# Filler matmuls on TensorE before four waits of the last stages left out, in a Perceiver layer on one core

## The chip, the core and the metric

The kernel runs on one core of a Trainium2 chip. The metric is the device time of one execution in microseconds (us), as the median of several executions. The profile is of one more execution, taken by the hardware profiler; its times are counted from the start of its span.

## What is computed

One layer on a state x of 128 rows x 512 columns and a context of 12544 rows x 512:

```
x = x + xattn(layernorm(x), ctx)          # 16 heads of 128, softmax over 12544 keys
x = x + lightning_attn(layernorm(x))      # 16 heads of 32, one chunk of 128 rows
x = x + ffn(layernorm(x))
# lightning_attn:
q, k, v = silu(x@Wq), silu(x@Wk), silu(x@Wv)
o = ((q k^T) * decay) v                   # per head
o = o * sigmoid(x@Wg1@Wg2);  o = rmsnorm per head * norm_w;  return o@Wo
# ffn: both products with ternary weights and rows rounded to 8 bits
h = gelu(silu(act_quant(rms_norm(x)) @ w1q^T + b1))
h = layer_norm(h) * ln_g + ln_b
return act_quant(rms_norm(h)) @ w2q^T + b2
```

## The kernel before, in words

Every engine has its own program, written out by hand, and each instruction that depends on another engine waits on a semaphore. Nothing is scheduled by a planner around the change: the order on TensorE is the order of the text in `block.tensor`.

The first 2017 us of the profile are the cross attention (the key and value products at L1097 and L1119). After it come these stages, all of which hang on one another:

- Heads of the cross attention, 16 times: VectorE normalises a head (L924), TensorE turns it (four f32 transposes, `transposes`, L1061), ScalarE copies it out (L684), TensorE multiplies by Wv (L1174) and Wo (L1181). Weights of the heads come by DMA (`bulk<-in_vo`).
- First norm: VectorE adds the residual (L939) and computes the layer norm with a guess of the reciprocal square root from GpSimd (L754 to L758, L458). TensorE waits for it (`ydone`), turns the result (L1061), ScalarE copies it (L688).
- Lightning attention: the gate's first product (L1206), Q and K (L1213, 64 matmuls of 128x128 f32), the gate's second product (L1217), V (L1220), scores (L1228), scores by V (L1237, 32 matmuls of 32 columns), and the residual put into `ps_c` by a product with the identity (L1240). VectorE then does the gate and the norm per head (L949 to L956). TensorE waits for it (`an_done`), turns the result, ScalarE copies it (L700), and TensorE multiplies by Wo (L1247).
- Third norm: ScalarE copies x2 (L702), VectorE computes the layer norm and rounds the rows to 8 bits (L987 to L979). TensorE waits for it (`f_q`), turns the rows in bf16 (L1061), ScalarE copies (L706), and TensorE multiplies by w1 (L1268, four groups `h_mm` of four matmuls 128x512 bf16). VectorE takes each group (L1003) and works on it with ScalarE: silu, gelu, statistics.
- Fourth norm: VectorE normalises the 2048 columns and rounds them in four parts (L1027 to L979, `h_norm`, `f2_q`). TensorE turns each part (L1061), ScalarE copies it (L724), and TensorE multiplies by w2 (`second`, L1256, 16 matmuls in all). VectorE adds it up (L1051), and the output is stored.

Before each of the four waits TensorE runs filler matmuls. `keep_warm(n)` issues n products of the identity in bf16 with 512 columns of the ternary weights, into the first bank of `ps_s`, which nobody reads before it is written again:

```
def keep_warm(n):
    for _ in range(n):
        mm(ps_s[:, 0:D], identb[:, :], tern[:, 0:D], start=True, stop=True)
```

The four calls: 14 ahead of the wait for `ydone`, 16 ahead of `an_done`, 28 ahead of `f_q`, and 24 behind the first wait for `h_norm`, ahead of the four waits for `f2_q`. They stand at L1196.

Of the kernel before, what the change touches and what calls it, by code (L numbers as in the profile page):

```python
# [6 lines left out]
D = 512  # L7
# [103 lines left out]
def perceiver_layer(nc, x_d, ctx_d, qk_d, vo_d, aw_d, wg1_d, wg2_d, w12_d, ld_d, normw_d, b1_d,  # L111
                    lng_d, lnb_d, b2_d, ident_d, diff_d, mask_d, out_d):
    es = ExitStack()
    with es:
        def sb(name, cols, dt=F32):
            return es.enter_context(nc.sbuf_tensor(name, [P, cols], dt))

        def pb(name, cols):
            return es.enter_context(nc.psum_tensor(name, [P, cols], F32))
# [20 lines left out]
        identb = sb("identb", P, BF16)  # L140
# [30 lines left out]
        tern = bulk[:, 0:WP * D].bitcast(BF16)  # L171
# [27 lines left out]
        def t_moving(k, lo, blk, c):  # L199
            start, stride, n, m, _, _ = window(k)  # L200
            return runs(bulk16, ((lo * 7 + blk) * 2 + c) * TW + start, stride, n, m)
# [9 lines left out]
        ps_s = pb("ps_s", 1024)  # L211
# [30 lines left out]
        def visit(k):  # L242

            return sum(e == STEPS[k][0] for e, _, _ in STEPS[:k])
# [108 lines left out]
        def _(sp):  # L353
# [62 lines left out]
            for k in range(1, NS + 1):  # L416
                turn_p(k - 1, 0)
                turn_p(k - 1, 1)
                for j, (_, _, at) in enumerate(LOADS):
                    if at == k + 1:  # L420
                        load_ctx(j)
                if 0 <= k - ABS_AT + 1 < 2 * WP:
                    load_w(k - ABS_AT + 1)
                if 0 <= k - QUANT_AT + 1 < 2 * WP:
                    load_w(2 * WP + k - QUANT_AT + 1)
                if 0 <= k - QUANT_AT - 1 < 2 * WP:
                    store_w(k - QUANT_AT - 1)
# [628 lines left out]
        def _(pe):  # L1056
            mm = nc.tensor.matmul
# [132 lines left out]
                    add_out(f - 1)  # L1190
            add_out(H - 1)

            def keep_warm(n):

                for _ in range(n):
                    mm(ps_s[:, 0:D], identb[:, :], tern[:, 0:D], start=True, stop=True)  # L1196


            pe.wait_ge(in_tern, 32)
            keep_warm(14)  # L1200
            pe.wait_ge(ydone, 2)
            transposes(ps_t, acc, KC, ident).then_inc(ytp, 1)
            pe.wait_ge(ytc, 2)
            yt = slot(1)
            for c in range(KC):
                last = mm(ps_a[0:AHD, 0:P], wg1[:, c * AHD:(c + 1) * AHD], yt[:, c * P:(c + 1) * P], start=(c == 0),  # L1206
                          stop=(c == KC - 1))
# [11 lines left out]
            for c in range(KC):  # L1219
                last = mm(ps_a[:, :], yt[:, c * P:(c + 1) * P], aw_v[:, c * D:(c + 1) * D], start=(c == 0),  # L1220
                          stop=(c == KC - 1))
# [16 lines left out]
                              slot(7)[:, h * AHD:(h + 1) * AHD], start=True, stop=True)  # L1238
            last.then_inc(ao_mm, 1)
            mm(ps_c[:, :], ident[:, :], x1[:, :], start=True, stop=False)  # L1240
            keep_warm(16)
            pe.wait_ge(an_done, 1)
            transposes(ps_t, slot(14), KC, ident).then_inc(at_mm, 1)
            pe.wait_ge(at_cp, 1)
            pe.wait_ge(in_aw2[2], 16)
            for c in range(KC):
                last = mm(ps_c[:, :], slot(1)[:, c * P:(c + 1) * P], aw_o[:, c * D:(c + 1) * D], start=False,  # L1247
                          stop=(c == KC - 1))
# [3 lines left out]
            def second(n):  # L1252
# [4 lines left out]
                              start=(c == 0), stop=(c == WP - 1), skip_group_check=True)  # L1257
                return last

            keep_warm(28)  # L1260
            pe.wait_ge(f_q, 1)
            transposes(ps_a[:, 0:D // 2].bitcast(BF16), slot(2)[:, 0:D // 2].bitcast(BF16), KC, identb).then_inc(f_tp, 1)
            pe.wait_ge(f_tc, 1)
# [5 lines left out]
                              tern[:, c * F + n * D:c * F + (n + 1) * D], start=(c == 0), stop=(c == KC - 1))  # L1269
                last.then_inc(h_mm, 1)  # L1270
            pe.wait_ge(h_norm, 1)
            keep_warm(24)
            for n in range(4):
                pe.wait_ge(f2_q, n + 1)
                src = slot(12 + n // 2)[:, (n % 2) * D // 2:(n % 2 + 1) * D // 2].bitcast(BF16)
# [61 lines left out]
```

## Time and profile before

| | us |
|---|---|
| median of 3 executions | 2171.31 (2171.03 to 2172.21) |
| the profiled execution's own time | 2166.53 |
| its span | 2164.7 |
| mean granted clock of TensorE over the span | 0.977 |
| TensorE busy | 2063.1 (95%) |
| VectorE busy | 1208.0 (56%) |
| ScalarE busy | 920.0 (42%) |

The granted clock is the share of the full 2.4 GHz: 1.00 is 2.4 GHz and 0.50 is 1.2 GHz. In a timeline a row is a run of like instructions, with its start, its length, and in brackets how long the engine had been idle ahead of it and what ended that. In the chain of waits a row is a piece of the path that ended last. In a table of windows "busy (x)" is the time and the number of instructions in the stretch, one that crosses its edge included. The table gives all of the span; the stages that the change touches lie behind 2087 us.

### The profile page before, as it was taken

How to read it: one execution, taken by the hardware profiler on the slowest of the kernel's cores; microseconds unless marked ns; L12 is line 12 of the kernel's file. 1: busy time of each engine (PE TensorE's matmuls, PEld its weight loads, DVE VectorE, ACT ScalarE, POOL GpSimd, SP SyncE). 2: the span in 40 equal slices, each digit the busy share in tenths (PEclk: the TensorE clock that was granted, in tenths of full speed). 3: DMA queues.
4: the chain of work that ended last, by engine and by line, in shares of the span. 5: the costliest groups of instructions: out<-in, count | busy, mean ns of one | idle time of the engine just before them, and what ended most of it. 6: DMA issues, size and time to landing. Idle time of an engine off the chain costs nothing.

```text
span 2164.7 us, 29322 instructions
## 1 busy us (share of the span) xinstructions
PE 2063.1 (95%) x11200; PEld 1112.1 (51%) x11200; DVE 1208.0 (56%) x2127; ACT 920.0 (42%) x1993; POOL 215.3 (10%) x241
## 2 busy tenths in 40 slices
PE   5599999999999999999999999999999999999686
PEld 4455555555555555555555555555555555555452
DVE  3455555556555556666766756555555565554326
ACT  3343445445454344444444444444444343443212
POOL 4401010001010010100000101010010100100001
PEclk8799999999999999999999999999999999999898
DMA  5243444444434435544545443343434343333730
GB/s 161 69 88 69 95 96 103 92 108 98 103 93 102 93 69 114 102 112 107 105 101 122 109 96 78 83 93 66 94 71 92 70 88 79 83 69 54 256 133 5
DMA packets 516698, 206.74 MB, mean 96 GB/s; under 512 B 418864, under 2 KB 502832, under 8 KB 515664
## 3 DMA queue, kind: packets, MB, share of 16 engines
q1 hardware_dynamic: 516560, 204.88, 41.9%
q8 instruction: 89, 1.46, 0.3%
q14 instruction: 49, 0.40, 0.1%
HBM read 97.59 MB, written 4.46 MB: 47 GB/s over the span
## 4 chain that ended last, share of the span: by engine, by line
PE 90%; DVE 4%; POOL 2%; DMA 2%; issue 1%; ACT 1%; SPq 0%; POOLq 0%; DVEq 0%; ACTq 0%
PE ps_s L1097 22%; PE ps_t L1097 17%; PE ps_b L1119 12%; PE ps_c L1119 12%; PE ps_a L1119 11%; PE ps_u L1119 11%; DMA bulk<-in_vo 1%; POOL acc L477 1%; PE ps_t L1174 1%; POOL stage L477 1%; PE ps_a L1076 0%; DVE pp L810 0%; PE ps_c L1181 0%; DMA acc<-in_qk 0%; PE ps_s L1213 0%
## 5 line engine op out<-in xcount | busy, mean ns | idle before, releaser
L1097 PE MATMUL ps_s<-bulk 128*128 128x384 f16 (+2 forms) x3264 | 579.0, 321 | 3.5 <-issue 3.2
L1097 PE MATMUL ps_t<-bulk 128*128 128x384 f16 (+2 forms) x2448 | 450.5, 321 | 14.9 <-ACT ps_t L638 10.1
L1097 PEld LDWEIGHTS ps_s<-bulk 128*128 128x128 f16 x3264 | 315.3, 98 | 216.5 <-issue 5.1
L477 POOL TENSOR_TENSOR stage<-stage 128x256 f32<-128x256 f32 x196 | 171.2, 873 | 1610.6 <-DMA stage<-in_ctx 1591.8
L1097 PEld LDWEIGHTS ps_t<-bulk 128*128 128x128 f16 x2448 | 233.9, 98 | 168.9 <-ACT ps_t L638 11.6
L638 ACT ACTIVATE ps_t<-ps_s 128x384 f32<-128x384 f32 (+2 forms) x136 | 62.9, 462 | 488.7 <-PE ps_s L1097 488.7
L1119 PE MATMUL ps_b<-nring,pt 128*128 128x512 f16 x1176 | 264.9, 379 | 1.0 <-DMA pt<-pp 1.0
L1119 PE MATMUL ps_u<-nring,pt 128*128 128x512 f16 x1176 | 265.0, 379 | 0.0
L1119 PE MATMUL ps_c<-nring,pt 128*128 128x512 f16 x1176 | 264.9, 379 | 0.0
L1119 PE MATMUL ps_a<-nring,pt 128*128 128x512 f16 x1176 | 264.9, 379 | 0.0
L810 DVE SCALAR_TENSOR_TENSOR pp<-prob,pp 128x768 f16<-128x768 f32 (+2 forms) x272 | 257.2, 987 | 0.1
L855 DVE TENSOR_TENSOR ps_t<-ps_t,part_e 128x384 f32<-128x384 f32 (+2 forms) x136 | 74.8, 550 | 244.9 <-PE ps_t L1097 244.8
L659 ACT ACTIVATE pp<-prob 128x768 f16<-128x768 f32 (+2 forms) x272 | 207.1, 812 | 3.0 <-DMA pt<-pp 3.0
L1119 PEld LDWEIGHTS ps_a<-nring,pt 128*128 128x128 f16 x1176 | 115.1, 98 | 138.8
L1119 PEld LDWEIGHTS ps_c<-nring,pt 128*128 128x128 f16 x1176 | 115.0, 98 | 138.9 <-DMA pt<-pp 0.3
L1119 PEld LDWEIGHTS ps_b<-nring,pt 128*128 128x128 f16 x1176 | 114.9, 98 | 132.4 <-DMA pt<-pp 1.5
L1119 PEld LDWEIGHTS ps_u<-nring,pt 128*128 128x128 f16 x1176 | 115.0, 98 | 131.2 <-DMA pt<-pp 0.3
L832 DVE SCALAR_TENSOR_TENSOR acc<-acc,alpha,ps_c 128x512 f32<-128x512 f32 x64 | 47.8, 748 | 194.1 <-PE ps_c L1119 194.1
L832 DVE SCALAR_TENSOR_TENSOR acc<-acc,alpha,ps_a 128x512 f32<-128x512 f32 x64 | 47.8, 747 | 192.8 <-PE ps_a L1119 192.8
L633 ACT ACTIVATE prob<-ps_s,nmax 128x768 f32<-128x768 f32 (+2 forms) x72 | 61.4, 853 | 194.4 <-DVE nmax L803 180.0
L799 DVE TENSOR_REDUCE mx<-ps_s 128x1 f32<-128x768 f32 (+2 forms) x136 | 126.0, 926 | 4.7
L799 DVE TENSOR_REDUCE mx<-ps_t 128x1 f32<-128x768 f32 (+2 forms) x136 | 125.0, 919 | 0.0
(185 smaller groups left out, 1600.0 us busy)
## 6 DMA issues: line engine op xcount, KB each, us to landing
stage<-in_ctx SPq DMA_DIRECT2D x392, 128.0 KB, 2.5
wst<-in_w SPq DMA_DIRECT2D x64, 256.0 KB, 3.3
acc<-in_qk SPq DMA_DIRECT2D x16, 512.0 KB, 4.6
bulk<-in_vo SPq DMA_DIRECT2D x16, 512.0 KB, 4.9
pt<-pp SPq DMA_TRANSPOSE x272, 4.0
tern_d<-wter SPq DMA_DIRECT2D x32, 128.0 KB, 3.1
bulk<-tern_d SPq DMA_DIRECT2D x2, 2048.0 KB, 16.1
nring<-in_aw SPq DMA_DIRECT2D x3, 1024.0 KB, 12.8
```

The lines of the kernel that those rows point to most:

```text
L477: nc.gpsimd.tensor_tensor(piece(t, dst), piece(t, a), piece(t, b), op).then_inc(done, 1)
L633: nc.scalar.activation(prob_of(k, g), scores_of(k, g), ACT.Exp, bias=nmax_of(k, g), scale=EXP_SCALE, accum_out=total).then_inc(exp_done[g], 1)
L638: nc.scalar.activation(bank_b(k), bank_a(k), ACT.Copy).then_inc(a_copied, 1)
L659: nc.scalar.activation(pp_part(k, g, 0), prob_of(k, g), ACT.Copy, scale=P_SCALE).then_inc(hi_done[g], 1)
L799: nc.vector.reduce_max(mx[:, g:g + 1], scores_of(k, g), AX.X).then_inc(mx_done, 1)
L810: nc.vector.scalar_tensor_tensor(pp_part(k, g, 1), prob_of(k, g), P_SCALE, pp_part(k, g, 0), ALU.mult, ALU.subtract).then_inc(lo_done[g], 1)
L832: nc.vector.scalar_tensor_tensor(slot(h), slot(h), alpha[:, h:h + 1], bank_u(k, g)[:, :], ALU.mult, ALU.add).then_inc(acc_done[g], 1)
L855: nc.vector.tensor_tensor(bank_d(k), bank_b(k), part_e[:, 0:cols(k)], ALU.add).then_inc(d_done, 1)
L1097: ins = mm(out, q_part(e, qlo, a)[:, c * P:(c + 1) * P], t_moving(k, tlo, b, c), start=(first and c == 0 and qlo == 0 and tlo == 0), stop= ...
L1119: ins = mm(bank_u(k, g)[:, :], pt[:, tile:tile + P], n_part(c, clo, half), start=(n == 0 and half == 0 and plo == 0 and clo == 0), stop=(n ...
L1174: last = mm(ps_t[:, (f % 2) * D:(f % 2) * D + HD], w[:, c * HD:(c + 1) * HD], ut[:, (f % 2) * D + c * P:(f % 2) * D + (c + 1) * P], start= ...
```

## The change

`keep_warm` and its four calls are left out. The waits, and all other instructions, stay in their order on every engine.

```diff
@@ -1190,14 +1190,7 @@
                     add_out(f - 1)
             add_out(H - 1)
 
-            def keep_warm(n):
-
-                for _ in range(n):
-                    mm(ps_s[:, 0:D], identb[:, :], tern[:, 0:D], start=True, stop=True)
-
-
             pe.wait_ge(in_tern, 32)
-            keep_warm(14)
             pe.wait_ge(ydone, 2)
             transposes(ps_t, acc, KC, ident).then_inc(ytp, 1)
             pe.wait_ge(ytc, 2)
@@ -1238,7 +1231,6 @@
                               slot(7)[:, h * AHD:(h + 1) * AHD], start=True, stop=True)
             last.then_inc(ao_mm, 1)
             mm(ps_c[:, :], ident[:, :], x1[:, :], start=True, stop=False)
-            keep_warm(16)
             pe.wait_ge(an_done, 1)
             transposes(ps_t, slot(14), KC, ident).then_inc(at_mm, 1)
             pe.wait_ge(at_cp, 1)
@@ -1257,7 +1249,6 @@
                               start=(c == 0), stop=(c == WP - 1), skip_group_check=True)
                 return last
 
-            keep_warm(28)
             pe.wait_ge(f_q, 1)
             transposes(ps_a[:, 0:D // 2].bitcast(BF16), slot(2)[:, 0:D // 2].bitcast(BF16), KC, identb).then_inc(f_tp, 1)
             pe.wait_ge(f_tc, 1)
@@ -1269,7 +1260,6 @@
                               tern[:, c * F + n * D:c * F + (n + 1) * D], start=(c == 0), stop=(c == KC - 1))
                 last.then_inc(h_mm, 1)
             pe.wait_ge(h_norm, 1)
-            keep_warm(24)
             for n in range(4):
                 pe.wait_ge(f2_q, n + 1)
                 src = slot(12 + n // 2)[:, (n % 2) * D // 2:(n % 2 + 1) * D // 2].bitcast(BF16)
```

## Rows read from the trace of the kernel before

**Rows 1.** Chain of waits behind 2087 us: start, us, engine, tile, line, count

```profile
2091.34 0.67 PE ps_t L1061 x4
...
2093.74 7.34 PE ps_s L1213 x64
...
2108.51 4.41 PE ps_u L1237 x32
...
2121.70 3.71 PE ps_c L1247 x8
...
2133.93 1.92 PE ps_s L1268 x8
...
2135.87 0.75 DVE acc L1003
...
2139.12 0.75 DVE acc L1003
...
2159.30 0.40 PE ps_s L1061 x4
2159.69 1.74 PE ps_c L1256 x8
```

**Rows 2.** Timeline of TensorE behind 2087 us: fillers and what follows them

```profile
2087.31 3.19 PE L1196 MATMUL ps_s<-bulk,identb 128*128 128x512 bf16 x14
...
2114.57 5.38 PE L1196 MATMUL ps_s<-bulk,identb 128*128 128x512 bf16 x16
...
2125.23 6.21 PE L1196 MATMUL ps_s<-bulk,identb 128*128 128x512 bf16 x28
2132.85 0.40 PE L1061 MATMUL ps_a<-identb,acc 128*128 128x128 bf16 x4 [1.41 <-DVE acc L979]
...
2147.87 7.50 PE L1196 MATMUL ps_s<-bulk,identb 128*128 128x512 bf16 x24 [10.31 <-DVE acc L1035]
2155.34 0.40 PE L1061 MATMUL ps_t<-identb,acc 128*128 128x128 bf16 x4
2156.66 0.40 PE L1061 MATMUL ps_t<-identb,acc 128*128 128x128 bf16 x4 [0.92 <-DVE acc L979]
```

**Rows 3.** Timeline of TensorE: idle stretches without fillers, elsewhere in the kernel

```profile
75.59 0.51 PE L1097 MATMUL ps_t<-bulk 128*128 128x128 f16 x6 [2.24 <-DVE ps_t L855]
...
124.57 3.79 PE L1097 MATMUL ps_s<-bulk 128*128 128x384 f16 x12 [3.17 <-issue]
...
2021.35 1.25 PE L1061 MATMUL ps_s<-ident,un 128*128 128x128 f32 x8 [3.85 <-DVE un L924]
...
2025.81 1.12 PE L1061 MATMUL ps_s<-ident,un 128*128 128x128 f32 x4 [0.98 <-DVE un L924]
...
2067.57 2.08 PE L1174 MATMUL ps_t<-ut,bulk 128*128 128x128 f32 x8 [7.23 <-DMA bulk<-in_vo]
...
2077.89 1.06 PE L1174 MATMUL ps_t<-ut,bulk 128*128 128x128 f32 x8
```

**Rows 4.** Windows of TensorE: us, PE busy (count), granted clock, DMA share, GB/s

```profile
77.00:78.00 1.00, 0.04 (x1) 0.50 0.65 131
...
124.60:125.00 0.40, 0.40 (x2) 0.67 0.00 0
...
128.00:129.00 1.00, 1.00 (x7) 0.92 0.77 204
...
2022.00:2023.00 1.00, 0.81 (x6) 0.77 0.97 410
...
2073.60:2073.80 0.20, 0.20 (x3) 0.63 1.09 430
...
2111.20:2111.40 0.20, 0.20 (x3) 0.74 0.00 0
...
2142.00:2142.20 0.20, 0.00 (x0) 0.54 0.00 0
...
2152.20:2152.40 0.20, 0.20 (x2) 0.86 0.00 0
```

## The prediction

> **What bounds the kernel now.** I first read the chain of waits behind 2087 us [rows 1]: to 2121.70 it goes through TensorE's own products (Q and K 7.34 us, scores by V 4.41 us, the product by Wo 3.71 us), later through VectorE with TensorE answering, and at the end through TensorE again (1.74 us for the last eight products). No filler stands in it. The timeline says why [rows 2]: the 14 fillers end at 2090.5, the 16 at 2119.95 and the 28 at 2131.44, each before its wait ends (the transposes of the third norm have 1.41 us of idle ahead of them, behind the fillers). Only the 24 last ones touch their successor: 2147.87 + 7.50 = 2155.37 against transposes at 2155.34. So the fillers cost next to nothing, and the question is what they hold up: the clock. The windows [rows 4] show the granted clock at one of two levels, 1.00 (2.4 GHz) or 0.50 (1.2 GHz).
>
> **How the clock falls.** A stop is the start of a row less its idle time. TensorE stopped at 73.35 and was idle 2.24 us [rows 3]; at 77.00 the clock was 0.50 [rows 4]. It stopped at 121.40, was idle 3.17 us [rows 3], and the mean of 0.67 between 124.60 and 125.00 [rows 4] puts the fall at 124.74, 3.3 us after the stop. It stopped at 2017.50, was idle 3.85 us [rows 3], and the mean of 0.77 from 2022 to 2023 [rows 4] puts the fall at 2022.54, 5.0 us after the stop and behind eight transposes. It stopped at 2137.56, which is 10.31 us ahead of 2147.87 [rows 2], and the clock fell at 2142.02 [rows 4], 4.5 us later. Not one of these idle times was survived.
>
> **How it rises.** Work began at 124.57 and the clock rose at 128.16, 3.6 us later; at 2067.57, rose at 2073.75, 6.2 us; at 2147.87 (the fillers themselves), rose at 2152.26, 4.4 us [rows 2 to 4]. I take the middle one, 4.4 us, and 3.6 and 6.2 as bounds. At 1.2 GHz the same eight products take 2.08 us against 1.06 [rows 3], so of 4.4 us half, 2.2 us, are lost (bounds 1.8 and 3.1). Four f32 transposes take 1.12 us at the low clock [rows 3] against 0.67 [rows 1]: 0.45 us more.
>
> **The change part by part.** It removes 82 matmuls with their weight loads, adds and moves nothing; the other engines' programs are the same, no DMA is touched, and the waits stay. Without the fillers the four idle stretches are:
>
> *First norm.* Idle from about 2087.4 (start of the fillers) to 2091.34 [rows 1, 2], 3.9 us, as long as the 3.85 us above [rows 3]. By the rows the fall comes 3.3 to 5.0 us after the stop, so before or after the transposes: I take half of 0.45, 0.2 us. Then come the gate's product and 64 of Q and K, without a pause, and the chain is TensorE's own: 2.2 us. **2.4 us**, bounds 1.8 and 3.5 if it falls at all.
>
> *Scores by V.* These 32 small products cost 4.41 us, and the clock falls at 2111.30 [rows 4], 2.8 us into them. At the full clock they would take 2.8 + 1.6/2 = 3.6 us, at the low one 7.2. The stage arrives later than before, and where the fall then comes no row shows. I take **0**, since the same products lead up to it; bounds -0.8 and +2.8.
>
> *Norm per head.* Idle over 5.4 us (the length of the 16 fillers) [rows 2], ahead of it those small products, with the clock already low: low for certain when work returns. The transposes cost 0.45 and the product by Wo 2.2: at the low clock throughout it would take some 3.5 us more, and it is on the path. **2.6 us**, bounds 2.2 and 4.0.
>
> *Third norm.* Idle 7.6 us (2125.23 to 2132.85) [rows 2], more than any of the stops survived. The four bf16 transposes take 0.40 us where f32 ones take 0.67, so I put them at half of 0.45: 0.2. VectorE reads the second group at 2135.87 as soon as eight matmuls from 2133.93 are done [rows 1]. The 28 fillers in 6.21 us give 0.22 us for one at 2.4 GHz, hence 0.43 at 1.2: eight are 1.7 us late. The last group is read only at 2139.12, and with the clock back after 4.4 us it is ready by then, so the later groups add nothing. **1.9 us**, bounds 1.7 and 2.7 (all sixteen at the low clock are ready 2 us after 2139.12).
>
> *Fourth norm.* Idle from 2137.56 to 2155.34. Here the fillers started cold too, and had the clock up 3 us before the rows came. Without them the first transposes (0.2 us late) are covered by VectorE, which gives the next part only at 2156.66. From there three blocks of transposes (0.5 us each at the low clock) and 16 products at 0.43 make 8.3 us of low-clock work, up to 2165 instead of 2161.4: 3.6 us if the clock stays low. If it rises 4.4 us after 2155.34, 5.4 us of this work are left and run in 2.7, end 2162.5; if 4.4 us after 2156.66, 3.9 are left, end 2163.0. **1.3 us**, bounds 0.9 and 3.6.
>
> **The sum** is 2.4 + 0 + 2.6 + 1.9 + 1.3 = 8.2 us. The profiled execution took 2166.53 us, so its like would take 2174.7. The median of the runs stands 4.8 us above it, at 2171.31; none of the four stages waits for a DMA, so I carry the sum over unchanged: **2179.5 us**.
>
> **The rivals.** *The clock survives the first norm.* Its idle is the shortest of the four, and the stop of 3.85 us [rows 3] kept the clock for 5.0 us. Then that term is gone: 5.8 us, 2177.1. Against it, there too the clock fell a moment later, and 2.24 us of idle sufficed at 73.35. Chance 0.17.
>
> *The clock comes back late or not at all in each stage.* The work there is short and broken by transposes and waits, and the 6.2 us of 2067.57 had transposes within. Then 3.5 + 0 + 4.0 + 2.4 + 3.6 = 13.5 us, 2184.8. Beside this stands a rule of the Trainium skill ("TensorE: Matmul & The Clock Gate", Part 4: PE-mode transpose): the full clock does not engage for transposes, which do not count as a busy TensorE in the same way. By that rule the last stage, in which transposes alternate with products, would be nearer to its 3.6 us than to my 1.3. The rise at 2073.75 came after a stretch with transposes in it, so the trace does not bear out the strong form. Chance 0.12.
>
> *Not slower.* In the last stage the fillers end at 2155.37 and the transposes wait for them. Where the clock rises 6.2 us after the restart instead of 4.4, the 24 fillers end 0.9 us later and hold up the path by as much, and leaving them out gives that back. This decides if the clock is still at 2.4 GHz when work returns in the other three stages, so that they lose nothing: 2170.4 to 2171.3. For it speaks only that a fall can come 5.0 us after a stop; against it are idle times of 5.4 and 7.6 us. Chance 0.06.
>
> *The low clock is mostly hidden*, because VectorE or ScalarE is late anyway in the last two stages and the rise comes early: 3 to 4 us, some 2175. The chain through TensorE [rows 1] speaks against it. Chance 0.05.
>
> **How the numbers follow.** The forecast keeps 0.60. The range leaves out the last two cases and the upper half of the late clock, together 0.17, and takes in the bounds of the terms where they don't all fall on one side: 2175.5 to 2183.0. A measurement of this kernel can tell about 0.2%, 4.3 us, from no change, that is 2175.6. Slower by more: nearly all of the forecast (0.58) and of the first rival (0.15), and the late clock (0.12): 0.85. Within 0.2%: the rest of those, the hidden case and most of the not-slower one: 0.13. Faster: 0.02.
>
> **What would show it.** In the profile of the changed kernel the granted clock should be 0.50 at the start of the Q and K products, of the product by Wo, of the product by w1 and of the last stage; the eight products by the attention's Wo should take about 6 us instead of 3.71, the Q and K products about 9.5 instead of 7.34, and VectorE should wait some 1.7 us longer for the second group of the product by w1. VectorE's own stretches between (the norms) should keep their length, and everything ahead of 2087 us its place. I am wrong if the clock is 1.00 at those places, if it is low and the stages still keep their length, or if the difference arises ahead of the first norm.

## The result and the profile after

The changed kernel takes 2175.57 us (median of 20 executions, 2172.68 to 2180.84) against 2171.03 us (20, 2168.47 to 2173.02) on the same chips: ratio 1.0023, 95% interval 1.0016 to 1.0030, which is 3.5 to 6.5 us slower. The forecast was 2179.5 us (8.2 us slower), with a range of 2175.5 to 2183.0: the measured median lies 3.9 us below the forecast and only 0.07 us inside the lower end of the range. The profiled execution of the changed kernel took 2173.32 us (span 2171.5 us) against 2166.53.

Ahead of 2087 us the programs are the same, and what differs there is the execution: the first head's transposes start 1.8 us later (2023.12 against 2021.35) and the first norm 0.9 us later (2088.41 against 2087.51). In all profiles of kernels that are alike up to there, the first norm starts between 2087.49 and 2090.84. Behind it the chain of waits of the kernel after reads as follows. The columns are start, length, engine, tile, line; L1206 was L1213, L1230 was L1237, L1239 was L1247, L1248 was L1256.

```profile
2092.34 0.64 PE ps_t L1061 x4
...
2093.65 1.91 PE ps_a L1199 x8
2095.57 8.05 PE ps_s L1206 x64
...
2111.05 4.18 PE ps_u L1230 x32
...
2122.65 1.13 PE ps_t L1061 x4
...
2124.46 5.33 PE ps_c L1239 x8
...
2141.86 0.75 DVE acc L1003
...
2162.65 0.61 PE ps_t L1061 x4
2163.26 1.71 PE ps_c L1248 x4
...
2165.39 0.87 PE ps_c L1248 x4
...
2166.49 1.74 PE ps_c L1248 x8
```

Against [rows 1], Q and K take 8.05 us instead of 7.34, the small products of the scores 4.18 instead of 4.41, the product by Wo 5.33 instead of 3.71, and the first four products by w2 1.71, twice their later 0.87. VectorE reads the second group of the product by w1 4.63 us behind the start of the turn, instead of 3.02. The timeline of TensorE shows the idle time that the fillers had covered, in brackets, against [rows 2]:

```profile
2092.34 0.63 PE L1061 MATMUL ps_t<-ident,acc 128*128 128x128 f32 x4 [3.96 <-DVE acc L758]
...
2122.65 1.12 PE L1061 MATMUL ps_t<-ident,acc 128*128 128x128 f32 x4 [5.58 <-DVE acc L956]
...
2137.23 0.61 PE L1061 MATMUL ps_a<-identb,acc 128*128 128x128 bf16 x4 [7.46 <-DVE acc L979]
...
2161.42 0.58 PE L1061 MATMUL ps_t<-identb,acc 128*128 128x128 bf16 x4 [17.87 <-DVE acc L979]
```

And the windows of TensorE (us, busy and count, granted clock, DMA share, GB/s) show the clock as in [rows 4]:

```profile
2093.50:2094.00 0.50, 0.35 (x2) 0.61 0.00 0
2097.00:2097.50 0.50, 0.50 (x6) 0.98 0.00 0
2124.00:2125.00 1.00, 0.54 (x1) 0.50 0.00 0
2127.50:2128.00 0.50, 0.50 (x2) 0.76 0.00 0
2137.00:2139.00 2.00, 0.68 (x5) 0.50 0.00 0
2141.00:2141.50 0.50, 0.50 (x3) 0.60 0.00 0
2161.00:2163.00 2.00, 0.93 (x8) 0.50 0.00 0
2165.00:2165.50 0.50, 0.50 (x6) 0.71 0.00 0
```

The clock is at 1.2 GHz from 2093.6 to 2097.0, from before the return of work at 2122.65 to 2127.7, and likewise to 2141.4 and to 2165.3: once in each of the four stages. (The moment of a fall or a rise is worked out from the mean clock of the window that it lies in.)

To compare executions I divide the stretch from the start of VectorE's residual add (L939) to the start of its last sum (L1051) at VectorE's results. Four pieces move, and the rest (the first norm, the norm per head and the third norm) is 17.8 us in every profile:

- attention: end of the first norm to VectorE's gate (Q and K, V, scores, small products)
- Wo: end of the norm per head to the statistics of x2 (turn, copy, product, copy)
- w1: third norm's rounded rows to the first rounded part of the fourth norm (VectorE's work of that norm included)
- last: from there to the last sum

| kernel (one profile each) | attention | Wo | w1 | last | whole stretch |
|---|---|---|---|---|---|
| before | 21.74 | 5.76 | 22.48 | 6.25 | 74.02 |
| before_again | 23.61 | 5.76 | 23.78 | 6.24 | 77.20 |
| after | **23.14** | **7.84** | **24.11** | **7.04** | 79.91 |
| after_again | **26.24** | **7.76** | **24.06** | **7.03** | 82.89 |
| no_first | **23.59** | 7.47 | 23.78 | 6.24 | 78.87 |
| no_second | 21.76 | **9.26** | 23.58 | 6.24 | 78.65 |
| no_third | 21.79 | 5.76 | **24.42** | 6.24 | 76.01 |
| no_fourth | 21.40 | 7.46 | 23.96 | **7.41** | 78.03 |
| turned_fill | 23.92 | 5.77 | 24.15 | 6.24 | 77.86 |
| heads_fill | 22.06 | 5.77 | 23.77 | 6.24 | 75.64 |
| heads_fill3 | 23.17 | 5.77 | 22.48 | 6.24 | 75.44 |
| full_fill | 21.95 | 6.22 | 22.49 | 6.25 | 74.70 |
| late_loads | 23.21 | 5.77 | 22.49 | 6.24 | 75.50 |
| late_all | 23.77 | 6.02 | 22.49 | 6.24 | 76.31 |

Bold: the piece has no fillers ahead of it. The stretches of after and before differ by 5.9 us; with the 0.9 us ahead of it, that is the 6.8 us between their profiled executions. The expectations below count some pieces from the turn's start instead: 21.68 us there is 21.74 here, 5.08 is 5.76 (with ScalarE's copy), 3.02 lies within the 22.48.

### The profile page after: what moved, and what is told of

Its sections match the earlier page's. It is cut to its first block, busy times and chain, and to the rows that moved or that the text cites. A ratio compares the mean times of both kernels' runs of the same rounds, so it can differ in the third digit from the quotient of the medians.

```text
span 2171.5 us, 29159 instructions
## 1 busy us (share of the span) xinstructions
PE 2048.8 (94%) x11117; PEld 1108.5 (51%) x11118; DVE 1207.4 (56%) x2127; ACT 919.3 (42%) x1993; POOL 214.3 (10%) x241
## 4 chain that ended last, share of the span: by engine, by line
PE 91%; DVE 3%; POOL 2%; DMA 2%; issue 1%; ACT 1%; SPq 0%; POOLq 0%; DVEq 0%; ACTq 0%
PE ps_s L1097 23%; PE ps_t L1097 17%; PE ps_b L1119 12%; PE ps_c L1119 12%; PE ps_u L1119 11%; PE ps_a L1119 11%; DMA bulk<-in_vo 1%; POOL acc L477 1%; PE ps_t L1174 1%; POOL stage L477 1%; PE ps_a L1076 0%; DMA acc<-in_qk 0%; PE ps_c L1181 0%; PE ps_s L1061 0%; PE ps_s L1206 0%
```

## The experiments

**One call left out at a time.** Each is the kernel before less one line. For no_first it is this one; for no_second, no_third and no_fourth it is `keep_warm(16)`, `keep_warm(28)` and `keep_warm(24)`.

```diff
-            keep_warm(14)
```

> Only the 14 fillers ahead of the first norm's wait are left out. Clock theory: idle of 3.9 us, the granted clock falls about when the transposes run and comes back 3.4 us later, so the stretch from the transposes to the gate (21.68 us before) takes 1 to 2 us more, and the other three stages keep their lengths (5.08, 3.02 and 6.25 us); the time is 1 to 2 us above before. Rival (the fillers matter by something other than the clock): the clock stays 1.00 and the stretch is still longer, or the loss turns up in a later stage.

> Only the 16 fillers ahead of the wait for the norm per head are left out. Clock theory: the piece from the transposes to the copy of x2 takes 7.1 us instead of 5.08 (transposes 1.12, product by Wo 5.3 us), +2.0 us in all, and the 28 fillers behind it restore the clock, so that the next stages keep their lengths. Rival: the piece keeps its length, or the loss is carried on into the third norm as well.

> Only the 28 fillers ahead of the third norm's wait are left out. Clock theory: VectorE reads the second group of the product by w1 1.6 us later (4.6 us behind the transposes' start instead of 3.0), the groups behind it add nothing, +1.6 us in all. Rival: sixteen matmuls at the low clock make the last group late, too: +2 us or more.

> Only the 24 fillers behind the first wait for h_norm are left out. Clock theory: the piece from the first rounded part to the last sum of VectorE takes 7.0 us instead of 6.25, +0.8 us; the clock comes back 3 to 4 us after the first transposes. Rival (transposes do not bring the clock back, as my late-clock case had it): the clock stays at 0.50 to the end and the piece is 3 us or more longer.

Measured (ratio to before, 95% interval): no_first 1.0008 (0.9997 to 1.0018), no_second 1.0016 (1.0006 to 1.0025), no_third 1.0002 (0.9992 to 1.0011), no_fourth 1.0006 (0.9996 to 1.0015). Only the second call alone is clear of noise; the four add up to 0.0032, against 0.0023 for all together, within their intervals. In the profiles the stage without its fillers is longer than in the first profile of before in each case (bold in the table), as the clock theory had it: by 1.9, 3.5, 1.9 and 1.2 us. Three of these are more than the theory's own numbers (2.0, 1.6 and 0.8 for the last three). The late clock of my prediction's rival did come in no_second: there it rose at 2128.61 only, so the eight products by Wo took 6.74 us, nearly all at 1.2 GHz. In no_third the clock rose 5.6 us after the first transposes of the stage, and VectorE read the second group 4.93 us after them (expected 4.6); the later groups added nothing. For no_fourth the rival fell: transposes and products together had the clock back 4.6 us after the first transposes (2161.38 to 2165.97), a little later than the 3 to 4 us expected.

But in three of the four the rest of the expectation failed: *other* stages, their fillers in place, did not keep the lengths of the first profile (only no_third has them all). In no_first the product by Wo, with its 16 fillers in place, took 5.40 us. The timeline and the windows of no_first show why:

```profile
2117.13 4.14 PE L1196 MATMUL ps_s<-bulk,identb 128*128 128x512 bf16 x16
2122.91 0.66 PE L1061 MATMUL ps_t<-ident,acc 128*128 128x128 f32 x4 [1.64 <-DVE acc L956]
2124.26 5.40 PE L1246 MATMUL ps_c<-nring,acc 128*128 128x512 f32 x8 [0.69 <-ACT acc L700]
```

```profile
2124.00:2125.00 1.00, 0.74 (x2) 1.00 0.00 0
2125.00:2128.00 3.00, 3.00 (x5) 0.50 0.00 0
2128.00:2129.00 1.00, 1.00 (x3) 0.79 0.00 0
```

The clock had come back about 1 us after these fillers began (3.6 us in before), so the same 16 took 4.14 us instead of 5.38 and ended 1.64 us ahead of the turn; 0.69 us of ScalarE's copy follow behind it, and the clock fell at 2125.0, some 0.75 us into the product. The other profiles bear this out. Of those with 16 fillers there (turned_fill with its transposes included), the two with 1.64 and 1.75 us of idle ahead of this turn (no_first, no_fourth) lost the clock in the product by Wo; the seven with 0.20 to 0.91 us kept it.

**Is that the kernel before, too?** Both kernels again, unchanged.

> The kernel before, unchanged, for a second profile. Theory (the fillers keep the clock only in some executions, since the idle left around them lets it fall too): from VectorE's residual add of the first norm to its last sum this takes more than the 74.0 us of the first profile, 75 to 78 us, with the product by w1 or by Wo at the low clock at its start and the small products of the scores at 4.0 to 6.7 us. Rival (the first profile is typical, the other losses came from the edits): 74.0 to 74.5 us.

> The changed kernel, unchanged, for a second profile. Its stretch from the residual add to the last sum took 79.9 us. Theory: 79 to 82 us here, with each of the four stages low at its start, and the time at low clock in them different from the first profile by up to 2 us a stage. Rival: 79.9 us again within 0.3, stage by stage.

The second profile of before has a stretch of 77.20 us, 3.2 more than the first, and the execution took 2171.13 us; the first took 2166.53. (Other executions of before have a median of 2171.03 us in the comparison with after and of 2169.64 us beside this run.) Of the 4.6 us between the two, 3.2 lie in the stretch and 1.4 ahead of it. Its windows of TensorE, first under the small products of the scores, then at the product by w1 with the 28 fillers ahead of it:

```profile
2111.00:2120.00 9.00, 9.00 (x33) 0.50 0.00 0
...
2137.00:2138.00 1.00, 0.78 (x4) 0.96 0.00 0
2138.00:2141.00 3.00, 3.00 (x9) 0.50 0.00 0
```

and the rows of its timeline there:

```profile
2136.13 0.40 PE L1061 MATMUL ps_a<-identb,acc 128*128 128x128 bf16 x4 [1.42 <-DVE acc L979]
2137.22 2.95 PE L1268 MATMUL ps_s<-bulk,prob 128*128 128x512 bf16 x8 [0.69 <-ACT prob L706]
```

The idle ahead of this turn is that of the first profile (1.41 us in [rows 2]), which kept the clock; this one lost it at 2137.9. The first window shows a second thing: the clock fell at 2110.6, under the 32 small products, which took 6.35 us instead of 4.41. The changed kernel's second profile has a stretch of 82.89 us, all four stages low at their starts, and differs from its first mostly in the attention piece (26.24 against 23.14). Its clock was low from 2092.2 to 2099.1 in the first stage, and rose 7.7 us after the first transposes. The stretch is longer than the 82 us that I had set as the upper end.

**Transposes as fillers.** The filler's 512 columns as four transposes of 128:

```diff
-                for _ in range(n):
-                    mm(ps_s[:, 0:D], identb[:, :], tern[:, 0:D], start=True, stop=True)
+                for i in range(4 * n):
+                    at = i % 4 * P
+                    nc.tensor.transpose(ps_s[:, 0:D // 2].bitcast(BF16)[:, at:at + P], tern[:, at:at + P], identb[:, :])
```

> Each filler matmul is replaced by four bf16 transposes 128x128 (same columns, TensorE as long busy). If transposes hold the clock like matmuls, all four stages keep the lengths of before (21.68, 5.08, 3.02, 6.25 us) and the time is that of before within 1 us. If they do not count (the rule of the Trainium skill, TensorE: Matmul & The Clock Gate, Part 4), the clock falls while they run, the stages take the lengths of the kernel without fillers (22.99, 7.16, 4.63, 7.04), and the time is 4 to 6 us above before.

Ratio 1.0001 (0.9991 to 1.0010). The windows of TensorE in the stretches in which it ran transposes as fillers:

```profile
2119.40:2121.40 2.00, 2.00 (x21) 0.50 0.00 0
2121.50:2122.00 0.50, 0.50 (x9) 0.77 0.00 0
...
2130.00:2137.00 7.00, 6.43 (x113) 1.00 0.01 2
...
2154.40:2159.00 4.60, 4.60 (x45) 0.50 0.00 0
2159.00:2159.50 0.50, 0.50 (x9) 0.72 0.12 33
2159.50:2162.00 2.50, 2.50 (x49) 1.00 0.00 0
```

From 2154.31 on only transposes run, and the clock comes back at 2159.28; from 2130 to 2137 they hold it. So these bf16 transposes count for the clock here, against the rule of the Trainium skill that the prediction weighed ("TensorE: Matmul & The Clock Gate", Part 4: PE-mode transpose). No run has f32 transposes alone. The lengths did not all come out as expected: the attention piece (23.92 us) and the w1 piece (24.15) are the longer ones, as in before_again, from falls at 2111.49 under the small products and at 2138.80 in the product by w1. The Wo piece and the last one have the lengths of before.

**Fillers led up to the ends of the waits.**

```diff
-            keep_warm(14)
+            keep_warm(17)
             pe.wait_ge(ydone, 2)
             transposes(ps_t, acc, KC, ident).then_inc(ytp, 1)
+            keep_warm(2)
...
             keep_warm(16)
+            pe.wait_ge(lna, 3)
+            keep_warm(6)
             pe.wait_ge(an_done, 1)
             transposes(ps_t, slot(14), KC, ident).then_inc(at_mm, 1)
+            keep_warm(2)
...
-            keep_warm(28)
+            keep_warm(33)
```

with two more behind the turn of the third norm.

> Before, with the fillers led up to the end of each wait (17 instead of 14; 6 more behind GpSimd's guess for the norm per head; 33 instead of 28) and two more behind each turn, while ScalarE copies. Theory: the clock is 1.00 through the product by Wo and the product by w1 in the profile (5.8 and 3.1 us for the two pieces), the stretch takes 74 to 76 us, what is left being the small products of the scores, and the time is 1 to 2 us below before. Rival: the clock still falls there, or the fillers themselves hold up the turns, and the time is that of before or above.

The clock did as expected in the profile: one fall under the small products at 2112.6, then 1.00 from 2119.4 through both products. These are windows of full_fill:

```profile
2088.90:2112.00 23.10, 22.64 (x156) 1.00 0.00 1
2112.00:2113.00 1.00, 1.00 (x10) 0.80 0.00 0
2119.00:2120.00 1.00, 1.00 (x5) 0.79 0.00 0
2120.00:2143.00 23.00, 18.92 (x82) 1.00 0.00 1
```

The time is 2169.16 us, ratio 0.9997 (0.9988 to 1.0006): the 1 to 2 us are neither shown nor excluded. The Wo piece was 6.22 us instead of 5.76, since the 22 fillers there ended 0.5 us after VectorE's result (2122.04) and held up the turn, as the rival had it: part of what is saved is given back.

**The clock in the stage ahead.** In the heads' stage TensorE waits for weights, 10.42 us ahead of 2045.83 and 7.23 us ahead of 2067.57 [rows 3], and works on at 1.2 GHz. The first of these rows in the timeline of before:

```profile
2045.83 2.08 PE L1174 MATMUL ps_t<-ut,bulk 128*128 128x128 f32 x8 [10.42 <-DMA bulk<-in_vo]
```

```diff
                 w = ring_vo[:, (f % 4) * SL:(f % 4 + 1) * SL]
+                for _ in range({4: 44, 9: 30}.get(f, 0)):
+                    mm(ps_a[:, :], identb[:, :], wter[:, 0:D], start=True, stop=True)
                 pe.wait_ge(in_vo[f % 4], 16 * (f // 4 + 1))
...
+            pe.wait_ge(w_quant, 2 * WP)
             turn(0)
```

heads_fill3 has 16 more into `ps_s` ahead of the first head, behind a wait for the last exponentials.

> Before, plus 44 and 30 fillers into ps_a ahead of the two waits of the heads' stage for weights (10.42 and 7.23 us of idle; the fillers take 9.5 and 6.5 at 2.4 GHz). Clock theory: the clock is 1.00 when the weights are there, instead of 0.50 for 4.0 and 6.1 us; +0 for the transfers, and 3 to 5 us faster than before. Rival: the transfers set the end of this stage, what TensorE gains it waits for the next weights, and the time moves by less than 2 us.

> As heads_fill, plus 16 fillers into ps_s in the idle 3.85 us ahead of the first head. Clock theory: 2.5 us of low clock are gained there, but the weights waited for next are limited by the DMA queue, so that little of it reaches the end: 0 to 1 us faster than heads_fill. Rival: the transfers start earlier by as much, 2 us or more faster than heads_fill.

Ratios 0.9993 (0.9983 to 1.0004) and 1.0008 (0.9999 to 1.0017): no gain is shown, and heads_fill3 did not come out faster than heads_fill, as I had expected by 0 to 1 us. The windows of heads_fill show the clock up where before had 0.51 and 0.68 in the same windows:

```profile
2040.00:2050.00 10.00, 7.17 (x37) 1.00 0.73 299
2060.00:2070.00 10.00, 7.85 (x40) 0.99 0.88 360
```

Yet the weights came at 2047.17 and 2068.68, 1.3 and 1.1 us later than in before, and the first norm began at 2087.41 (before: 2087.51). This stage seems to hang on the queue, so that a clock gained is only a longer wait; the next run tests that.

**The queue relieved.** That points to the loads themselves: 4 MB of ternary weights and 4 MB of attention weights stand ahead of the weights of heads 4 to 15, and 3.5 MB of broadcast vectors behind those of head 8 (the expectation below says 4.25 MB; the five loads in the profile are three of 1024 KB and two of 256 KB).

```diff
-            sp.dma_start(aw_q, aw_d[0]).then_inc(in_aw, 16)
...
+                if f in (5, 7, 9, 11):
+                    n = (f - 5) // 2
+                    sp.dma_start((aw_q, aw_k, aw_v, aw_o)[n], aw_d[n]).then_inc(([in_aw] + in_aw2)[n], 16)
-                if f == 8:
+                if f == H - 1:
...
+                    for n in range(2):
+                        sp.dma_start(tern[:, n * WP * D:(n + 1) * WP * D].rearrange("p (n d) -> p n d", d=D),
+                                     tern_d[n * WP:(n + 1) * WP].rearrange("n p d -> p n d")).then_inc(in_tern, 16)
```

The fillers read `wter` here, and `in_tern` is waited for ahead of the product by w1.

> Before, with the loads that the heads' stage does not need (4 MB ternary weights, 4 MB attention weights, 4.25 MB broadcast vectors) moved behind or between the heads' own weights on the queue, and the fillers reading wter instead of tern. Theory (in the stage between 2017 and 2087 us the queue sets the end, which is why TensorE's clock did not matter there): the waits of 10.4 and 7.2 us go, 15 to 20 us faster. Rival (that stage hangs on the clock and the chain of a head): under 5 us faster.

2149.83 us, ratio 0.9908 (0.9895 to 0.9922): 20 us faster, at the upper end of what I had expected. The first norm begins at 2070.34, and no wait of TensorE for weights in this stage is longer than 0.9 us in the profile. So the stage did hang on the order of the loads. In late_loads the clock is low from 2020.8 to 2031.1, at the first heads (window of late_loads), and with the queue relieved it may lie on the path:

```profile
2021.00:2031.00 10.00, 8.01 (x30) 0.50 0.15 59
```

late_all adds the fillers of full_fill and 17 ahead of the first head:

```diff
+            pe.wait_ge(w_quant, 2 * WP)
+            pe.wait_ge(exp_done[0], NS)
+            for _ in range(17):
+                mm(ps_s[:, 0:D], identb[:, :], wter[:, 0:D], start=True, stop=True)
             turn(0)
```

> late_loads with the longer fillers of full_fill and 17 fillers ahead of the first head (idle 3.84 us there, clock low from 2020.8 to 2031.1 in late_loads). Theory: with the queue relieved TensorE's clock counts in the heads' stage, 2 to 4 us faster than late_loads, that is 22 to 24 us faster than before. Rival: the weights' loads, 7.2 us from issue to landing in late_loads, still set that stage, and it is the time of late_loads within 1 us.

2147.72 us, ratio 0.9894 (0.9880 to 0.9909), the best of all kernels run; the clock is 1.00 from 2020 to 2068 in its profile, and the first norm begins at 2066.78, 3.6 us earlier than in late_loads; the stretch behind it is 0.8 us longer (76.31 against 75.50). The medians differ by 2.1 us, as the theory wants, but the two intervals overlap. So the step from late_loads to late_all is seen in one profile of each and is not shown by the times.

## Why the prediction was right, and where its size was off

**Direction and mechanism: right, step by step.** No filler stood on the path, and taking them out made no stage start earlier. The idle stretches came out at 3.96, 5.58, 7.46 and 17.87 us (forecast 3.9, over 5.4, 7.6 and 17.8). The clock was at 0.50 at the four places named, VectorE's norms kept their lengths, and the loss arose in the four stages named. Two sizes given as signs came out smaller: the Q and K products took 8.05 us (forecast about 9.5, which put the whole loss on them, though part of it falls on the gate's product, 1.91 us instead of 1.06) and the product by Wo 5.33 (about 6). VectorE's wait for the second group grew by 1.6 us (forecast 1.7). Of the rivals, "not slower" and "the clock survives the first norm" are out: without the 14 fillers the clock fell in all three profiles (after, after_again, no_first). A clock as late as the rival's 6.2 us behind the start of the products appeared in two places: no_second at the product by Wo (8.0 us after the first transposes, 6.2 after the product's start) and after_again in the first stage (7.7 and 6.3 us); it did not appear in the last stage, where it rose 3.8 to 4.6 us after the first transposes. What the not-slower rival lived on was seen in part: in before_again the 24 fillers ended 0.9 us after the first rounded part and held up its turn by some 0.6 us, but the last piece was 6.24 us all the same, so nothing of it reached the end. The rival of the hidden clock (some 2175 us) came nearer to the measured 2175.57 than the forecast did, but by its number only: in the last two stages, where it wanted the loss hidden, the pieces grew by 1.7 and 0.9 us on the mean, against the 1.9 and 1.3 of the forecast.

**The terms.** Against the first profile of before, which is what the sum was made against, and as means over the profiles without the fillers in question:

| term | forecast | first profile after | mean without the fillers |
|---|---|---|---|
| first norm and small products | 2.4 + 0 | 1.4 | 2.6 (3 profiles) |
| norm per head (Wo) | 2.6 | 2.1 | 2.5 (3) |
| third norm (w1) | 1.9 | 1.6 | 1.7 (3) |
| fourth norm (last) | 1.3 | 0.8 | 0.9 (3) |
| sum | 8.2 | 5.9 | 7.7 |

In the first profile after, the low clock of the first stage lasted 3.4 us (2093.6 to 2097.0), and in the other three stages it ended 5.1, 4.2 and 3.9 us after the first transposes. I had let the 4.4 us begin with the products in the first two stages; at the product by Wo it rose 3.3 us behind the product's start here, and 6.2 us behind it in no_second. On the mean the sum is right to within 0.5 us, and part of that is luck: the first row's 2.6 is the mean of 1.4, 4.5 and 1.9, and its small products, which I had put at 0, gave -0.2, +1.5 and -0.4.

Two slips of the working change little. In the fourth norm, with a rise at 2159.74, 3.1 of the 8.3 us of work are done and 5.2 are left, not 5.4, which ends at 2162.4. And the late-clock sum takes 2.4 us for the third norm where the bound given is 2.7.

**The step that failed is the last one: "I carry the sum over unchanged".** I took the four stages of the first profile as what the fillers give, and they are not. That execution took 2166.53 us, 4.8 below the median, which the prediction noted and put aside. (Against the second profile of before, 1.4 us of such a distance lie ahead of the stretch; the rest is in it.) Over the eight profiles that have a given call in its old form (before, before_again, heads_fill, heads_fill3, late_loads and the three that lack another call), the clock fell all the same in two of eight at the product by Wo (7.46 and 7.47 us) and in five of eight at the product by w1 (23.58 to 23.96). Their means are 22.34 (attention), 6.19, 23.29 and 6.24 us, together 58.06, against 56.23 in the first profile. The kernels without fillers have 24.32, 8.29, 24.20 and 7.16, together 63.97. The difference is 5.9 us, inside the measured 3.5 to 6.5; what is missing from 7.7 is the 1.8 us that kernels with the fillers lose as well, on the mean. Leaving out the 28 fillers alone costs 0.9 us by these means, which fits with no_third staying within noise. These are means of eight and of three profiles, of kernels that differ elsewhere, worked out after the result. They agree with the measured difference; they do not prove it to the microsecond, and what brings 5.9 down to the measured 4.5 is open.

How long the low clock lasts the runs show only in samples. In the stages without fillers it ended 3.8 to 8.0 us after the first transposes. Why a given execution falls at one place and not at another has an answer at the product by Wo only, where the idle ahead of it differs. At the product by w1 all eight profiles of the means have 1.41 or 1.42 us of idle ahead of the turn and 0.69 behind it, and three kept the clock while five lost it: that stays open.

## What to carry to other kernels

In full_fill and late_all, where the fillers reach up to the end of the wait and fill the short wait behind the turn too, the clock stayed up through both products; shorter fillers kept it in some executions only. A count fitted in one profile falls short in another, as the fillers themselves run faster when the clock is up early. Before an edit worth a few microseconds is costed against a profile, look where that execution stands among the runs: here the one profiled was 4.8 us below the median, and part of what it showed as kept was lost in most of the other profiles. And ask of a slow clock whether the stage hangs on the engine at all: in the heads' stage a full clock gave nothing that could be measured, the order of the loads gave 20 us, and only then did the clock seem to matter.

## What the runs showed of the hardware

- Transposes alone (bf16, 128x128) brought the clock back (turned_fill, 4.97 us after 2154.31) and held it from 2130 to 2137.
- In all 14 profiles the clock falls under the 32 small products (128x32, f32), during which TensorE shows no idle time: in before at 2111.30, in before_again at 2110.6, in turned_fill at 2111.49. Where fillers followed, it stayed low for 3.4 us (no_first) to 10.2 us (before_again, 2110.6 to 2120.85), with TensorE at work. The 32 took 4.03 us (no_first) to 6.65 us (turned_fill).
- Short idle times can lose it as well: in no_first 1.64 and 0.69 us, with one turn of 0.66 us between, went ahead of a fall. The same gaps need not end alike: 1.41 and 0.69 us at the product by w1 kept the clock in before and lost it in before_again (1.42 and 0.69).
